# Every second expert's down projection as three single-pass products of high and low parts

## The chip, the core and the metric

The kernel runs on one NeuronCore of a Trainium2 chip. The metric is device time in microseconds from launch to end. TensorE (PE) multiplies, ScalarE (ACT) applies functions and copies, VectorE (DVE) and GpSimd (POOL) work elementwise, SyncE (SP) issues most of the transfers.

## What is computed

Eight sequences of 512 tokens with 128 features go through an attention layer and a mixture of experts, each followed by a residual sum and a layer norm:

```python
x = _layernorm(x + attention(x, w_qkv))            # 16 heads of 8
...
combine = ...                                      # top 8 of 16 experts, scaled, else 0
hg = jnp.einsum('bsd,eid->bsei', x, w_gate)
hu = jnp.einsum('bsd,eid->bsei', x, w_up)
h = jax.nn.silu(hg) * hu
ye = jnp.einsum('bsei,edi->bsed', h, w_down)
y = jnp.einsum('bsed,bse->bsd', ye, combine)
y = y + shared expert (gate, up, silu, down)
x = _layernorm(x + y)
```

All 16 experts are computed for every token and weighted with `combine`. All arithmetic is float32.

## The kernel before

There are two stages. The attention stage runs over the 8 batches and ends with the routing of the first batch; a barrier of all engines lies between the stages. The feed-forward stage (`feed_forward`) runs over 8 batches: `body` is written out for the first and the last, with a loop over the six between. Tiles have features or hidden units on the 128 partitions and the 512 tokens of a batch in the free dimension.

A batch has 18 steps (`STEPS`), 0 to 17. "Net" 0 is the shared expert, nets 1 to 16 are the experts. In step s:

- PE makes `gate` and `up` of net s (L1197), each as three matmuls of type fp32r, which PE takes in a single pass: low weights by high x, high weights by high x, high weights by low x. "High" is a value rounded to fp32r, "low" is the rest. Then it makes the down projection of net s - 4 (`LAG`, L1227), one float32 matmul into `ps_y`, which the trace shows as two records. The down projections of nets 14 to 16 come in steps 0 to 2 of the next batch.
- ACT turns `ps_gate` into `silu` (L1115).
- DVE multiplies it with `ps_up` (in PSUM) into `gated` (L1167).
- POOL multiplies `gated` with the routing weights into `hidden` (L1085); both inputs are in SBUF.

The other work of a batch is written between these by step number. DVE: moments of the next batch (step 0), its layer norm `x` (step 2, L305), the sum `y_sum` (step 6), routing in three parts (`select_experts`, steps 7, 9, 11), the layer norm `result` of the batch before (step 13, L305). POOL: `scale` (steps 1 and 7), a copy of x1 (step 3, L324). ACT: the copy of y (step 3), of x1T (step 5), `decay` (step 7, with two table loads), `combine_T` (step 14).

The end of a batch is a hand-over. After `up` of net 16, ACT rounds the transposed x1 of the next batch into `x1T_high` (L344, step 17); DVE then subtracts to get `x1T_low` (L349); PE meanwhile makes the down projections of nets 12 and 13, and then step 0 of the next batch, which is ordered so that four matmuls need only `x1T_high` and the fifth is the first to need `x1T_low`:

```python
if s == 0:
    pe.wait_ge(r.x1T_split, b + 1)
```

Each engine works through its own instructions in the order written, waiting on semaphores. The rings are `silu` and `gated` 3 deep, `hidden` 6 deep, `ps_gate` 2, `ps_up` 3.

Of the kernel before, what the change touches and what calls it, by code (L numbers as in the profile page):

```python
# [124 lines left out]
NETS = EXPERTS + 1  # L125
ROUTE_SCALE = 2.826
# [25 lines left out]
def build(nc, x, xT, w_qkv, w_nets, w_downs, gate_wT, expert_bias, out):  # L152
    q_rows = nc.dram_tensor("q_rows", [HEADS, ROWS, SEQ], F32).ap()
    k_rows = nc.dram_tensor("k_rows", [HEADS, ROWS, SEQ], F32).ap()
    shift_rows = nc.dram_tensor("shift_rows", [2, GROUP * TILES, P], F32).ap()
    combine_rows = nc.dram_tensor("combine_rows", [EXPERTS, SEQ], F32).ap()
    x_tiles = x.rearrange("b (t p) d -> p (b t) d", p=P)
    out_tiles = out.rearrange("b (t p) d -> p (b t) d", p=P)

    with ExitStack() as whole:  # L160
        def keep(name, shape, dt=F32):
            return whole.enter_context(nc.sbuf_tensor(name, shape, dt))


        stream = keep("stream", [P, BATCHES * TILES, HIDDEN])
        nets_high = keep("nets_high", [P, NETS, 2, P], F32R)
        nets_low = keep("nets_low", [P, NETS, 2, P], F32R)
        nets_down = keep("nets_down", [P, NETS, P])
        ident = keep("ident", [P, P])
        r = RouteState(nc, whole, combine_rows)  # L170
        c = ContextState(nc, whole)
        attention(nc, r, c, stream, nets_high, nets_low, nets_down, ident, x_tiles, xT, w_qkv,
                  w_nets, w_downs, gate_wT, expert_bias, q_rows, k_rows, shift_rows)
        feed_forward(nc, r, c, stream, nets_high, nets_low, nets_down, ident, out_tiles)


class RouteState:


    def __init__(self, nc, ctx, combine_rows):  # L180
# [36 lines left out]
        self.downs_loaded = sem("downs_loaded")  # L217
        self.moments_ready = [sem("moments_in"), sem("moments_out")]
# [216 lines left out]
def attention(nc, r, c, stream, nets_high, nets_low, nets_down, ident, x_tiles, xT, w_qkv,  # L435
              w_nets, w_downs, gate_wT, expert_bias, q_rows, k_rows, shift_rows):
    with ExitStack() as ctx:
# [167 lines left out]
        def _(pool):  # L605
# [39 lines left out]

            def body(b, first=False, last=False):
                for g in range(GROUPS):
# [15 lines left out]
                    if g == 3:  # L663
                        add_context(pool, c, stream, 2 * b, b, 0)
                    if first and g > 0:
                        split_net(g - 1)
                        load_net(g)
                    elif not first and not last and g in (1, 3):
                        split_net(2 * b + 1 + g // 2)
                        load_net(2 * b + 2 + g // 2)  # L670
                    elif last and g < 2:
                        split_net(NETS - 2 + g)
                        if g == 0:
                            load_net(NETS - 1)

# [318 lines left out]
def feed_forward(nc, r, c, stream, nets_high, nets_low, nets_down, ident, out_tiles):  # L994
# [6 lines left out]
    def before(s, ring):  # L1001
# [4 lines left out]
        return (0, n) if n >= 0 else (-1, n + STEPS)  # L1006

    with ExitStack() as ctx:  # L1008
# [14 lines left out]
        result = sb("result", [P, TILES, HIDDEN])  # L1023

# [10 lines left out]
        hidden_done = sem("hidden_done")  # L1035
        down_done = sem("down_done")
# [65 lines left out]
        def _(act):  # L1102
# [4 lines left out]

            def body(b, first=False, last=False):
                for s in range(STEPS):
# [6 lines left out]
                    if s == STEPS - 1 and not last:  # L1116
# [3 lines left out]
                        round_x1T(act, r)  # L1120

# [16 lines left out]
        def _(dve):  # L1138
# [13 lines left out]

            def gate_up(b, s, first):
# [15 lines left out]
            def body(b, first=False, last=False):  # L1169
                for s in range(STEPS):  # L1170
                    if s <= LAST:
                        gate_up(b, s, first)
                    if s == STEPS - 1 and not last:
                        split_x1T(dve, r, b + 1)
                    if s == LN_IN - 1 and not last:
# [20 lines left out]
        def _(pe):  # L1196
# [30 lines left out]
            def down(b, n, first):  # L1227
                if n == 0:
                    pe.wait_ge(gated_done, NETS * b + 1)
                    if not first:  # L1230
                        pe.wait_ge(y_copied, b)
                else:
# [29 lines left out]
            pe.wait_ge(r.downs_loaded, DMA)  # L1262
            turn_context(pe, c, ident, 2 * BATCHES - 1, 1, c.ps_turned)
# [39 lines left out]
```

## Time and profile before

| | |
|---|---|
| median of 3 runs | 723.49 us (723.25 to 724.71) |
| the profiled execution | 725.11 us, of which the span of its instructions is 723.4 us |
| granted TensorE clock, mean | 0.966 |
| busy in the span | PE 687.6, PE's weight loads 361.9, DVE 515.3, ACT 415.6, POOL 321.2 us |

Busy time is the union of an engine's instructions; the ends of matmuls are modelled. The chain that ended last is followed back from the last instruction, at each step to what released it; its pieces lie end to end, so their lengths are the time that each took on the path. A row of the timeline gives an instruction's start and its duration, waits inside the instruction included. The feed-forward stage begins at 393 us.

### The profile page before, as it was taken

The page shows a single profiled execution, that of the slowest core. Times are in us where ns is not written, and L with a number is a line of the kernel's source. Part 1 is how long each engine was busy: PE and PEld are TensorE (multiplying, and loading weights), DVE is VectorE, ACT ScalarE, POOL GpSimd, SP SyncE. Part 2 cuts the span into 40 slices and gives each one's busy share as a digit, 9 for nine tenths or more (in the row PEclk, how much of TensorE's full clock was granted, in tenths as well). Part 3 has the DMA queues.
Part 4 walks back from the last instruction along what each step waited for, and adds up shares of the span by engine and source line. Part 5 has one row for each costly group of instructions (what it writes and reads, how often), then busy time and mean ns, then how long its engine had stood idle before and what let it go on. Part 6 is the DMA issues. An engine that isn't in the chain of part 4 may idle for free. (4 is left out here: it accounts for less than half of the span.)

```text
span 723.4 us, 13286 instructions
## 1 busy us (share of the span) xinstructions
PE 687.6 (95%) x3494; PEld 361.9 (50%) x3494; DVE 515.3 (71%) x1085; ACT 415.6 (57%) x779; POOL 321.2 (44%) x371
## 2 busy tenths in 40 slices
PE   2899999999999999999997999999999999999995
PEld 1343333433434334343323767666676767676662
DVE  1889988999999999999953546557565655656343
ACT  2068877988879888787886424334343434334321
POOL 3033342423424252252230756665565646666563
PEclk8569999999999999999999999999999999999998
DMA  6832251422414233241105023050606032140600
GB/s 184 257 98 89 84 156 34 140 70 82 155 53 148 68 100 110 82 137 52 46 5 202 33 108 128 22 227 0 248 0 245 3 145 103 50 198 9 239 1 29
DMA packets 34279, 74.89 MB, mean 104 GB/s; under 512 B 4144, under 2 KB 13488, under 8 KB 30032
## 3 DMA queue, kind: packets, MB, share of 16 engines
q1 hardware_dynamic: 33440, 72.38, 29.1%
q0 software_dynamic: 816, 2.23, 1.1%
q8 instruction: 11, 0.18, 0.1%
q14 instruction: 12, 0.10, 0.0%
HBM read 58.61 MB, written 15.99 MB: 103 GB/s over the span
## 5 line engine op out<-in xcount | busy, mean ns | idle before, releaser
L743 ACT ACTIVATE probs<-ps_k 128x512 f32<-128x512 f32 x500 | 262.6, 605 | 51.7 <-PE ps_k L849 47.5
L786 DVE TENSOR_REDUCE maxima<-ps_bank 128x1 f32<-128x512 f32 x384 | 245.4, 682 | 27.5 <-PE ps_bank L842 22.4
L1085 POOL TENSOR_TENSOR hidden<-gated,weights 128x512 f32<-128x512 f32 x128 | 167.0, 1311 | 124.2 <-DVE gated L1167 108.4
L1115 ACT ACTIVATE silu<-ps_gate 128x512 f32<-128x512 f32 x136 | 81.3, 598 | 176.9 <-PE ps_gate L1209 176.6
L1167 DVE TENSOR_TENSOR gated<-silu,ps_up 128x512 f32<-128x512 f32 x128 | 87.0, 685 | 105.2 <-PE ps_up L1209 69.7
L842 PE MATMUL ps_bank<-k_aug,q_aug 32*128 32x512 f32 x384 | 147.9, 513 | 12.5 <-DMA q_aug<-q_rows 8.8
L849 PE MATMUL ps_k<-q_aug,k_aug 32*128 32x512 f32 x500 | 154.2, 489 | 4.0 <-ACT probs L743 2.2
L862 PE MATMUL ps_ctx<-probs,v_ones 128*32 128x512 f32 x1024 | 138.8, 614 | 0.9 <-ACT probs L743 0.9
L1234 PE MATMUL ps_y<-hidden,nets_down 128*128 128x512 f32 x272 | 137.1, 591 | 0.0
L849 PEld LDWEIGHTS ps_k<-q_aug,k_aug 32*128 32x128 f32 x500 | 64.0, 185 | 124.3 <-ACT probs L743 107.2
L1206 PE MATMUL ps_gate<-x1T_high,nets_low 128*128 128x512 f32 x136 | 96.5, 710 | 0.0
L618 POOL TENSOR_TENSOR shift<-shift_raw,ones 16x128 fp32r<-16x128 f32 x31 | 13.8, 445 | 180.5 <-ACT shift_raw L711 180.5
L786 DVE TENSOR_REDUCE maxima<-ps_turned 128x1 f32<-128x512 f32 x128 | 87.2, 681 | 3.5 <-PE ps_bank L842 1.9
L842 PEld LDWEIGHTS ps_bank<-k_aug,q_aug 32*128 32x128 f32 x384 | 61.0, 191 | 27.6 <-DVE maxima L786 14.8
L842 PE MATMUL ps_turned<-k_aug,q_aug 32*128 32x512 f32 x128 | 65.0, 508 | 1.3
L1234 PEld LDWEIGHTS ps_y<-hidden,nets_down 128*128 128x128 f32 x272 | 51.3, 189 | 15.6 <-issue 3.8
L1209 PE MATMUL ps_gate<-x1T_low,nets_high 128*128 128x512 f32 x136 | 53.6, 394 | 0.0
L1209 PE MATMUL ps_gate<-x1T_high,nets_high 128*128 128x512 f32 x136 | 53.6, 394 | 0.0
L1209 PE MATMUL ps_up<-x1T_low,nets_high 128*128 128x512 f32 x136 | 53.4, 393 | 0.0
L1206 PE MATMUL ps_up<-x1T_high,nets_low 128*128 128x512 f32 x136 | 53.2, 391 | 0.0
L1209 PE MATMUL ps_up<-x1T_high,nets_high 128*128 128x512 f32 x136 | 53.2, 391 | 0.0
L1209 PEld LDWEIGHTS ps_gate<-x1T_high,nets_high 128*128 128x128 f32 x136 | 25.8, 189 | 24.9 <-issue 24.5
(117 smaller groups left out, 648.9 us busy)
## 6 DMA issues: line engine op xcount, KB each, us to landing
weights<-combine_rows SPq DMA_DIRECT2D x32, 1024.0 KB, 7.5
k_aug<-k_rows SPq DMA_DIRECT2D x32, 256.0 KB, 2.7
q_aug<-q_rows SPq DMA_DIRECT2D x32, 256.0 KB, 2.9
q_rows<-qk_high SPq DMA_DIRECT2D x16, 256.0 KB, 2.9
k_rows<-qk_high SPq DMA_DIRECT2D x16, 256.0 KB, 3.6
net_raw<-w_nets POOLq DMA_DIRECT2D x17, 128.0 KB, 2.4
xT_sb<-xT SPq DMA_DIRECT2D x8, 256.0 KB, 2.9
q_rows<-qk_low SPq DMA_DIRECT2D x8, 256.0 KB, 3.1
```

The source lines that it names most:

```text
L618: pool.tensor_tensor(shift[:, 0, :], shift_raw[:], r.ones[0:GROUP * TILES, 0:P], ALU.mult).then_inc(shift_high, 1)
L743: act.activation(probs[:, t, h, :], score_slot(i, last)[:], ACT.Exp, scale=ATT_SCALE).then_inc(exp_done, 1)
L786: dve.tensor_reduce(maxima[:, parity, TILES * h + t:TILES * h + t + 1], bank("q", (i - UNIT * AHEAD) % SCORES)[:], AX_X, ALU.max).then_inc ...
L842: return pe.matmul(bank("q", (i - UNIT * AHEAD) % SCORES)[:], q_aug[rows, g, t * P:(t + 1) * P], k_aug[rows, g, :], start=True, stop=True) ...
L849: return pe.matmul(score_slot(i, last)[:], k_aug[rows, g, t * P:(t + 1) * P], q_aug[rows, g, :], start=True, stop=True).then_inc(scores_k, 1)
L862: last = pe.matmul(ps_ctx[32 * h:32 * (h + 1), :], v_ones[:, g, t, h, :], probs[:, t, h, :], start=opens, stop=closes)
L1085: pool.tensor_tensor(hidden[:, s % RING, :], gated[:, s % UP_RING, :], r.weights[:, e, :], ALU.mult).then_inc(hidden_done, 1)
L1115: act.activation(silu[:, s % UP_RING, :], ps_gate[s % 2][:], ACT.Silu).then_inc(silu_done, 1)
L1167: dve.tensor_tensor(dst, silu[:, s % UP_RING, :], ps_up[s % UP_RING][:], ALU.mult).then_inc(gated_done, 1)
L1206: pe.matmul(dst[:], nets_low[:, s, j, :], r.x1T_high[:], start=True, stop=False)
L1209: return pe.matmul(dst[:], nets_high[:, s, j, :], x[:], start=False, stop=stop)
L1234: pe.matmul(ps_y[:], nets_down[:, n, :], hidden[:, n % RING, :], start=n == 0, stop=n == LAST).then_inc(down_done, 1)
```

## The change

For the odd nets 1, 3, ..., 15 the down projection is made as `gate` and `up` are: three fp32r matmuls. That needs the weights and `hidden` of these nets in high and low parts.

```diff
+            def split_downs():
+                odd = nets_down[:, 1:, :].rearrange("p (j two) d -> p j two d", two=2)[:, :, 0, :]
+                ones = r.ones[:, 0:P].unsqueeze(1).to_broadcast([P, SPLITS, P])
+                pool.wait_ge(r.downs_loaded, DMA)
+                pool.tensor_tensor(downs_high[:], odd, ones, ALU.mult).then_inc(r.downs_high_made, 1)
+                pool.wait_ge(r.downs_high_made, 1)
+                pool.tensor_tensor(downs_low[:], odd, downs_high[:].bitcast(F32), ALU.subtract
+                                   ).then_inc(r.downs_split, 1)
...
+                    if last and g == 3:
+                        split_downs()
...
+    def splits(s):
+        n = s - 2
+        return n > 0 and n % 2 == 1
...
+            def round_hidden(b, n, first):
+                j = n // 2
+                act.wait_ge(hidden_done, EXPERTS * b + n)
...
+                act.copy(hidden_high[:, j % SPLIT_RING, :], hidden[:, n % RING, :]).then_inc(hidden_highs, 1)
...
                         round_x1T(act, r)
+                    if splits(s):
+                        round_hidden(b, s - 2, first)
...
+            def split_hidden(b, n):
+                j = n // 2
+                dve.wait_ge(hidden_highs, SPLITS * b + j + 1)
+                dve.tensor_tensor(hidden_low[:, j % SPLIT_RING, :], hidden[:, n % RING, :],
+                                  hidden_high[:, j % SPLIT_RING, :].bitcast(F32), ALU.subtract
+                                  ).then_inc(hidden_split, 1)
...
                         split_x1T(dve, r, b + 1)
+                    if splits(s):
+                        split_hidden(b, s - 2)
...
+                elif n % 2 == 1:
+                    j = n // 2
+                    high, low = hidden_high[:, j % SPLIT_RING, :], hidden_low[:, j % SPLIT_RING, :]
+                    pe.wait_ge(hidden_highs, SPLITS * b + j + 1)
+                    pe.matmul(ps_y[:], downs_low[:, j, :], high, start=False, stop=False)
+                    pe.matmul(ps_y[:], downs_high[:, j, :], high, start=False, stop=False)
+                    pe.wait_ge(hidden_split, SPLITS * b + j + 1)
+                    pe.matmul(ps_y[:], downs_high[:, j, :], low, start=False, stop=False).then_inc(down_done, 1)
+                    return
...
+            pe.wait_ge(r.downs_split, 1)
             turn_context(pe, c, ident, 2 * BATCHES - 1, 1, c.ps_turned)
```

`splits(s)` holds in the odd steps 3 to 17: ACT and DVE handle net s - 2 right behind their work on net s, two steps before PE's down projection of it. In step 17 ACT rounds `x1T_high` first and `hidden_high` of net 15 behind it.

PE, the first batch, step 5: the end of `up` of net 5, the down projection of net 1, the transposes of x1. Before:

```order
L1206 MATMUL ps_up<-x1T_high,nets_low 128x512
L1209 MATMUL ps_up<-x1T_high,nets_high 128x512
L1209 MATMUL ps_up<-x1T_low,nets_high 128x512
L1234 MATMUL ps_y<-hidden,nets_down 128x512
L331 MATMUL ps_route<-ident,x 128x128 x4
```

After:

```order
L1254 MATMUL ps_up<-x1T_high,nets_low 128x512
L1257 MATMUL ps_up<-x1T_high,nets_high 128x512
L1257 MATMUL ps_up<-x1T_low,nets_high 128x512
L1284 MATMUL ps_y<-hidden_high,downs_low 128x512
L1285 MATMUL ps_y<-hidden_high,downs_high 128x512
L1287 MATMUL ps_y<-hidden_low,downs_high 128x512
L338 MATMUL ps_route<-ident,x 128x128 x4
```

One float32 matmul has become three of fp32r, with the same neighbours.

DVE, the first batch, steps 11 to 17: the third part of the routing (`chosen` to `combine`), the `gated` of nets 12 to 16, and `x1T_low`. In the other batches `result` (4 instructions) stands behind `gated` of net 13 as well. Before:

```order
L393 TENSOR_TENSOR chosen<-struck,select 128x64
L395 TENSOR_TENSOR picked<-chosen,score 128x64
L397 TENSOR_REDUCE total<-picked 128x4
L399 RECIPROCAL inverse_total<-total 128x4
L401 SCALAR_TENSOR_TENSOR combine<-picked,inverse_total 128x64
L1167 TENSOR_TENSOR gated<-silu,ps_up 128x512 x5
L349 TENSOR_TENSOR x1T_low<-x1T,x1T_high 128x512
```

After, behind the subtraction of net 9:

```order
L400 TENSOR_TENSOR chosen<-struck,select 128x64
L402 TENSOR_TENSOR picked<-chosen,score 128x64
L404 TENSOR_REDUCE total<-picked 128x4
L406 RECIPROCAL inverse_total<-total 128x4
L408 SCALAR_TENSOR_TENSOR combine<-picked,inverse_total 128x64
L1213 TENSOR_TENSOR gated<-silu,ps_up 128x512 x2
L1195 TENSOR_TENSOR hidden_low<-hidden,hidden_high 128x512
L1213 TENSOR_TENSOR gated<-silu,ps_up 128x512 x2
L1195 TENSOR_TENSOR hidden_low<-hidden,hidden_high 128x512
L1213 TENSOR_TENSOR gated<-silu,ps_up 128x512
L356 TENSOR_TENSOR x1T_low<-x1T,x1T_high 128x512
```

Each subtraction (of nets 11 and 13 here) stands between `gated` of its step and the extra work of that step; the one of net 15 follows `x1T_low`.

## Rows read from the trace of the kernel before

**Rows 1.** The page: busy time; the granted PE clock in 40 slices.

```profile
PE 687.6 (95%) x3494; PEld 361.9 (50%) x3494; DVE 515.3 (71%) x1085; ACT 415.6 (57%) x779; POOL 321.2 (44%) x371
...
PEclk8569999999999999999999999999999999999998
```

**Rows 2.** The page: the chain that ended last, by engine.

```profile
PE 45%; DVE 0%; POOLq 0%; ACT 0%; issue 0%; DVEq 0%; POOL 0%
```

**Rows 3.** A stretch: its us, busy (x) of PE, PEld, DVE, ACT, POOL; clock.

```profile
440.00:720.00 280.00, 275.28 (x1053) 186.50 (x1052) 155.89 (x408) 99.07 (x158) 165.97 (x143) 1.00 0.25 97
```

**Rows 4.** The chain in order of time, 607 to 613 us: start, us, what.

```profile
610.68 0.86 PE ps_y L1234 x2
611.54 0.23 PE ps_gate L1206
611.78 0.47 PE ps_gate L1209 x2
...
612.94 0.86 PE ps_y L1234 x2
```

**Rows 5.** The chain, 590 to 634 us: two batch ends.

```profile
590.97 1.72 PE ps_y L1234 x4
...
602.18 0.86 PE ps_y L1234 x2
...
631.34 1.72 PE ps_y L1234 x4
```

**Rows 6.** Single lines: count, shortest, median and longest in ns.

```profile
L349 DVE TENSOR_TENSOR x1T_low<-x1T,x1T_high x8: 682/684/693, 377.6 to 672.5; 128x512 fp32r<-128x512 f32 x8
...
L344 ACT CAST x1T_high<-x1T x8: 610/618/618, 376.9 to 671.8; 128x512 fp32r<-128x512 f32 x8
...
L1085 POOL TENSOR_TENSOR hidden<-gated,weights x128: 1262/1290/1666, 398.4 to 711.2; 128x512 f32<-128x512 f32 x128
```

**Rows 7.** Timeline, 618 to 634 us: start, us, what.

```profile
620.47 0.22 DVE L393 TENSOR_TENSOR chosen<-struck,select 128x64 f32<-128x64 f32 x1
...
620.63 1.29 POOL L1085 TENSOR_TENSOR hidden<-gated,weights 128x512 f32<-128x512 f32 x1 [0.94 <-DVE gated L1167]
620.76 1.24 DVE L395 TENSOR_TENSOR picked<-chosen,score 128x64 f32<-128x64 f32 x1
...
622.89 0.69 DVE L1167 TENSOR_TENSOR gated<-silu,ps_up 128x512 f32<-128x512 f32 x1
...
624.96 2.09 DVE L305 TENSOR_SCALAR result<-y_sum,moments,scale 128x128 f32<-128x128 f32 x4
...
625.13 1.33 POOL L1085 TENSOR_TENSOR hidden<-gated,weights 128x512 f32<-128x512 f32 x1 [0.19 <-DVE gated L1167]
...
626.97 0.67 DVE L1167 TENSOR_TENSOR gated<-silu,ps_up 128x512 f32<-128x512 f32 x1
```

**Rows 8.** Timeline of VectorE, 626 to 640 us: the end of a batch.

```profile
631.54 0.69 DVE L1167 TENSOR_TENSOR gated<-silu,ps_up 128x512 f32<-128x512 f32 x1 [1.56 <-POOL hidden L1085]
632.14 0.68 DVE L349 TENSOR_TENSOR x1T_low<-x1T,x1T_high 128x512 fp32r<-128x512 f32 x1
```

**Rows 9.** Timeline of GpSimd, same stretch.

```profile
632.30 1.66 POOL L1085 TENSOR_TENSOR hidden<-gated,weights 128x512 f32<-128x512 f32 x1 [0.95 <-DVE gated L1167]
```

**Rows 10.** Timeline of ScalarE, 589 to 606 us: the copy of y.

```profile
600.64 0.58 ACT L1106 COPY yT<-ps_y 128x512 f32<-128x512 f32 x1
```

**Rows 11.** Timeline of VectorE and the chain at 403 us: the first batch.

```profile
402.95 1.87 DVE L1167 TENSOR_TENSOR gated<-silu,ps_up 128x512 f32<-128x512 f32 x3
...
403.00 0.86 PE ps_y L1234 x2
```

**Rows 12.** Timeline at 385 to 394 us, and the halving of a net.

```profile
385.25 0.72 POOL L278 TENSOR_TENSOR stream<-stream,context 128x256 f32<-128x256 f32 x1 [10.91 <-DVE context L267]
...
393.27 0.63 PE L253 MATMUL ps_turned<-ident,context_T 128*128 128x128 f32 x4 [1.11 <-PEq L437]
...
L641 POOL TENSOR_TENSOR nets_high<-net_raw,ones x17: 716/731/740, 58.5 to 362.2; 128x256 f32 x12, 128x256 fp32r<-128x256 f32 x5
```

More of the change, by code:

```diff
@@ L125 @@
 NETS = EXPERTS + 1
+SPLITS = EXPERTS // 2
+SPLIT_RING = 4
 ROUTE_SCALE = 2.826
@@ L168, in build @@
         nets_down = keep("nets_down", [P, NETS, P])
+        downs_high = keep("downs_high", [P, SPLITS, P], F32R)
+        downs_low = keep("downs_low", [P, SPLITS, P], F32R)
         ident = keep("ident", [P, P])
@@ L171, in build @@
         c = ContextState(nc, whole)
-        attention(nc, r, c, stream, nets_high, nets_low, nets_down, ident, x_tiles, xT, w_qkv,
+        attention(nc, r, c, stream, nets_high, nets_low, nets_down, downs_high, downs_low, ident, x_tiles, xT, w_qkv,
                   w_nets, w_downs, gate_wT, expert_bias, q_rows, k_rows, shift_rows)
-        feed_forward(nc, r, c, stream, nets_high, nets_low, nets_down, ident, out_tiles)
+        feed_forward(nc, r, c, stream, nets_high, nets_low, nets_down, downs_high, downs_low, ident, out_tiles)
 class RouteState:
@@ L217, in __init__ @@
         self.downs_loaded = sem("downs_loaded")
+        self.downs_high_made = sem("downs_high_made")
+        self.downs_split = sem("downs_split")
         self.moments_ready = [sem("moments_in"), sem("moments_out")]
@@ L432, in load_weights, with attention @@
                  ).then_inc(r.weights_loaded[i], DMA)
-def attention(nc, r, c, stream, nets_high, nets_low, nets_down, ident, x_tiles, xT, w_qkv,
+def attention(nc, r, c, stream, nets_high, nets_low, nets_down, downs_high, downs_low, ident, x_tiles, xT, w_qkv,
               w_nets, w_downs, gate_wT, expert_bias, q_rows, k_rows, shift_rows):
@@ L991, in _, with feed_forward @@
             weigh_values(UNITS - 1, GROUPS - 1, TILES - 1, None)
-def feed_forward(nc, r, c, stream, nets_high, nets_low, nets_down, ident, out_tiles):
+def feed_forward(nc, r, c, stream, nets_high, nets_low, nets_down, downs_high, downs_low, ident, out_tiles):
     STEPS = NETS + 1
@@ L1023, in feed_forward @@
         result = sb("result", [P, TILES, HIDDEN])
+        hidden_high = sb("hidden_high", [P, SPLIT_RING, SEQ], F32R)
+        hidden_low = sb("hidden_low", [P, SPLIT_RING, SEQ], F32R)
         ps_gate = [psum("ps_gate0", [P, SEQ]), psum("ps_gate1", [P, SEQ])]
@@ L1035, in feed_forward @@
         hidden_done = sem("hidden_done")
+        hidden_highs = sem("hidden_highs")
+        hidden_split = sem("hidden_split")
         down_done = sem("down_done")
@@ L1106, in copy_y @@
                 act.copy(yT[:], ps_y[:]).then_inc(y_copied, 1)
+            def round_hidden(b, n, first):
+                j = n // 2
+                act.wait_ge(hidden_done, EXPERTS * b + n)
+                if j >= SPLIT_RING:
+                    act.wait_ge(down_done, NETS * b + n - 2 * SPLIT_RING + 1)
+                elif not first:
+                    act.wait_ge(down_done, NETS * (b - 1) + n + 2 * (SPLITS - SPLIT_RING) + 1)
+                act.copy(hidden_high[:, j % SPLIT_RING, :], hidden[:, n % RING, :]).then_inc(hidden_highs, 1)
             def body(b, first=False, last=False):
```

## The prediction

> **What bounds the kernel now.** I read the page first: PE is busy 95% of the span, the other engines at most 71%, and its granted clock is at full speed in all slices of the second half [rows 1]. Busy alone proves nothing, since the ends of matmuls are modelled, so I went to the chain that ended last: PE holds it for 45% of the span, which is the whole feed-forward stage, and every other engine has 0% [rows 2]. By stretches, in the loop batches PE is busy 275.3 of 280 us at clock 1.00, DVE 155.9, ACT 99.1, POOL 166.0 [rows 3]. The chain in order of time shows a step without extras as PE work end to end: from one down projection to the next 612.94 - 610.68 = 2.26 us, of which the float32 product takes 0.86; the fp32r products behind it take 0.23 and, two together, 0.47 [rows 4]. A batch takes 631.34 - 590.97 = 40.37 us [rows 5]. So in this stage time taken from PE is time won, until another engine is late.
>
> **What the change removes and adds on PE.** 64 float32 down projections (8 nets, 8 batches) of 0.86 us become 64 times three fp32r products of the same shape as those of gate and up, 3 x 0.23 = 0.69 us [rows 4]. That is 0.17 a product, 1.36 a batch, 64 x 0.17 = 10.9 us. Both sides: if the three went at the rate of the slowest fp32r piece, 0.24, it would be 0.14 x 64 = 9.0 us; if the step's remainder, 2.26 - 0.86 = 1.40 for six, held a cost of 0.03 that comes only with the float32 neighbour, 0.20 x 64 = 12.8. I take 10.9, since the pieces are even. The two extra semaphore waits of each product cost nothing when satisfied: the first products of gate and up carry such waits too, and their pieces are 0.23 like the others.
>
> The Trainium skill (FP8 and Floating Point Precision, TensorE Precision Notes) says that true float32 takes four passes through the array. By that rule a pass here is 0.86 / 4 = 0.215 us, and three of these would save 13.8 us; the trace has fp32r products at 0.23, so I stay with the rows.
>
> **What it adds elsewhere.** *ACT*: 64 roundings of 0.62 us, as x1T_high [rows 6]. ACT is busy 99 of 280 us, and the rounding in step s waits for the hidden of net s - 2, which POOL normally finishes some 2 us before. Behind it are queued the copy of y (step 3), of x1T (step 5), decay (step 7) and the next silu. The tightest is the copy of y: it moves from 600.64 to about 601.0 and is done by 601.6, while PE's down projection of net 0, at 602.18 before, asks for it at 602.0 [rows 5, 10]. So zero. *DVE*: 64 subtractions of 0.68 us, as x1T_low [rows 6], 5.5 us on 22.5 a batch: it stays under the 39 us of a batch. *POOL*: the weights are halved once. 256 columns take 0.73 us [rows 12], 512 take 1.29 [rows 6], so 1024 about 1.29 + 2 x 0.56 = 2.4, twice that is 4.8 us. It starts when the sum at 385.25 ends, 385.97, and is done by 390.8; PE begins the new stage at 393.27 [rows 12]. Zero, with 2.5 us of cover; at twice the duration it would cost 2.4 us.
>
> **Where something can get late.** The subtraction reads two SBUF tensors, as POOL's multiply does, and these shut each other out. At 620.47 chosen, on 128x64, took 0.22 us; at 620.76 picked, of the same size, took 1.24, until POOL's hidden of 620.63 was over; at the end of a batch hidden took 1.66 instead of 1.29 beside x1T_low [rows 6 to 9]. The gated product has one input in PSUM and takes 0.67 to 0.69 throughout [rows 7, 8]. The Trainium skill (SBUF, State Buffer; SBUF: two separate sides) speaks of an exclusive lock that is held for the whole instruction, by a VectorE operation with two SBUF inputs or by a GpSimd one; the trace agrees, with the 1.24.
>
> *First batch.* Steps 0 to 3 have no down projections, so PE comes early to net 1: its product starts at 403.00 [rows 11], the third part at 403.46. On DVE gated of net 3 follows the layer norm of step 2 at 402.95 (three of them in 1.87, 0.62 apart), the subtraction of net 1 at 403.57, done at 404.25. With 0.07 for the signal (a gated to its hidden) PE stands until 404.3: **0.85 us lost, once**.
>
> *Ends of the batches 1 to 6*, the ones with routing, result and hand-over. Occupancy is about 0.62 for a gated or a subtraction, 1.25 for a POOL multiply. I assume that whoever waits gets the port when the holder is done: result at 624.96 let POOL in at 625.13 between its four parts [rows 7]. In the times of the trace at 618 to 632 us:
> - Step 11: PE is 5 x 0.17 = 0.85 ahead by the end of it, gated of net 11 starts at 619.2, and the subtraction of net 9 behind it is done by 620.7. That pushes the routing's last part behind POOL's multiply of net 11, 620.7 to 621.95. From there chosen and picked take 0.25 each and the rest the 0.89 that lay between the end of picked (622.0) and 622.89 [rows 7]: gated of net 12 comes at 623.35 instead of 622.89, and its hidden, 0.76 behind and 1.25 long, is done at 625.35.
> - Step 13: the subtraction of net 11 waits for that, ends 625.96; POOL takes net 13 until 627.2; only then result (0.8 for its rest); gated of net 14 at 628.0 instead of 626.97 [rows 7], its hidden 628.75 to 630.0.
> - Step 15: gated of net 15 at 628.6; the subtraction of net 13 waits until 630.0, done 630.65. PE asks for it at 632.20 + 0.46 - 7 x 0.17 = 631.47. In time.
> - Step 16, 17: gated of net 16 at 630.65 (PE's products are ready at 631.54 - 1.19 = 630.35 [rows 8]); POOL has net 15 from 630.65 to 631.9; x1T_low 631.9 to 632.58. PE asks for it after its two down projections and four products: 631.34 + 1.72 + 0.92 - 8 x 0.17 = 632.62 [rows 5]. Before, it had 1.16 us to spare (632.82 against 633.98); now none.
>
> So the stall is zero by the sum, but with no reserve. Each of a dozen handovers is good to some hundredths. I take 0.15 us in each of 6 batches, 0.9 us; the bounds are 0 and what the rivals give. The last batch has neither routing nor hand-over, and the tail behind PE's last product is unchanged.
>
> **Sum.** Against the profiled execution, 725.11 us (span 723.4 and 1.7 around it): 725.11 - 10.9 + 0.85 + 0.9 = 715.95, that is 9.15 less. It was 1.6 above the median of the runs; on the median, 723.49 - 9.15 = **714.3 us**.
>
> **Rivals.**
> 1. *The collisions cost a real stall at each hand-over*, 0.5 to 1.0 us in 6 batches, 3 to 6 us in place of 0.9. For it: no reserve, and one further collision (0.6 to 1.25 us) on the way from step 9 to 17 is enough. Against: once PE has lost 0.5 us, all that follows has 0.5 more. 716.4 to 719.4 us.
> 2. *POOL goes on with its next multiply while DVE waits* (two ready multiplies back to back keep the port). Then each subtraction of steps 9 to 15 lets two of them pass: net 9's ends at 623.1, routing gives gated of 12 and 13 by 625.8, multiplies 12 and 13 run until 627.8, the subtraction of net 11 until 628.4, result until 629.3, gated of 14 and 15 until 630.5, multiplies 14 and 15 until 632.55, the subtraction of net 13 until 633.2: 1.8 us after PE's 631.47, and x1T_low 0.2 more. 6 x 2.0 = 12.0 us: 723.49 - 10.9 + 0.85 + 12.0 = 725.4, **slower**. It decides from 1.7 us a batch ((10.9 - 0.85) / 6). Against: rows 7 show POOL let in between DVE's parts, which speaks for taking turns; no row shows DVE waiting with two multiplies ready.
> 3. *The three products take as long as the float32 one* (0.86): then 723.5 to 726, no gain. Against: the same form stands next to it at 0.23. For it only that ps_y takes all three accumulating, as ps_gate does.
> 4. *The step keeps only what the even rate gives*, 0.20 a product, and no stall: 723.49 - 12.8 + 0.85 = 711.5.
>
> **Chances.** Forecast with stalls under 0.4 us a batch (713.2 to 715.8): 0.50. Rival 1: 0.29. Rival 2: 0.06. Rival 3 or a partial form that ends within 0.2%: 0.05. Rival 4: 0.10. The range reaches from rival 4 past most of rival 1: 711.3 to 720.0. A measurement can tell about 0.2%, 1.4 us, from no change. Faster: 0.50 + 0.29 + 0.10 = 0.89; within: 0.05; slower: 0.06.
>
> **What the profile after would show.** In the chain, odd down projections as three pieces with 0.69 in sum, steps alternating 2.26 and 2.09, a loop batch of 39.0 to 39.2 us. One pause of about 0.85 us before the third product of net 1 in the first batch, put down to DVE. DVE subtractions at 0.68 where alone and up to 1.3 longer beside a multiply; hidden up to 0.6 longer. At each hand-over x1T_low ending within some tenths of PE's fifth product. A wait of PE on ACT, or a steady wait on hidden_low in the loop batches, would prove my schedule wrong; pieces of 0.29 would prove the product's price wrong.

## The result, and the profile after

| | before | changed | ratio (95% interval) |
|---|---|---|---|
| median of the runs made side by side, us | 724.1 (723.25 to 728.98) | 717.32 (716.75 to 719.25) | 0.9873 (0.9826 to 0.9919) |
| profiled execution, us (span) | 725.11 (723.4) | 717.01 (715.3) | |
| feed-forward stage, us | 723.4 - 393.27 = 330.1 | 715.3 - 394.38 = 320.9 | |
| loop batch, us | 40.37 | 39.07 | |

The changed kernel is 1.3% faster by the ratio; the two medians alone differ by 0.9%, and a second, longer series gave 1.05% (below). The forecast was 714.3 us, between 711.3 and 720.0. The stage is measured from its first transposes (the row of L253 in [rows 12], of L260 below) to the end of the span, the batch from one copy of y to the next.

The page after: busy time, the granted clock in 40 slices, and the chain by engine (answers to [rows 1, 2]).

```profile
PE 678.9 (95%) x3558; PEld 373.8 (52%) x3558; DVE 580.4 (81%) x1149; ACT 448.0 (63%) x843; POOL 348.0 (49%) x373
...
PEclk8569999999999999999999999999999999999998
...
PE 44%; DVE 1%; POOLq 0%; issue 0%; ACT 0%; DVEq 0%; POOL 0%
```

In a chain, "issue" is time in which the engine waited for nothing that the profile shows, and a q behind an engine's name stands for its sequencer. PE is still the chain, 8.7 us less busy, and DVE has 65 us more. The loop batches as one stretch (answers to [rows 3]; the stretch is 272 us, as the loop is shorter):

```profile
440.00:712.00 272.00, 267.16 (x1113) 197.30 (x1111) 214.15 (x465) 128.44 (x216) 185.85 (x143) 1.00 0.26 102
```

DVE went from 0.56 of the stretch to 0.79. That is much more than 64 subtractions of 0.68, as the single lines show (answers to [rows 6]; count, then shortest/median/longest in ns):

```profile
L1113 POOL TENSOR_TENSOR hidden<-gated,weights x128: 1267/1304/1752, 399.5 to 703.3; 128x512 f32<-128x512 f32 x128
```

```profile
L1195 DVE TENSOR_TENSOR hidden_low<-hidden,hidden_high x64: 677/1146/1779, 404.7 to 703.7; 128x512 fp32r<-128x512 f32 x64
```

The median subtraction takes 1.15 us, 0.68 alone. The rest is time beside POOL's multiply, which in turn takes 1.49 on average (1.31 before). The chain in order of time, in the batches of 600 to 630 us and where they meet (answers to [rows 4, 5]):

```profile
606.22 0.23 PE ps_y L1284
606.45 0.24 PE ps_y L1285
606.69 0.23 PE ps_y L1287
...
608.31 0.86 PE ps_y L1291 x2
```

```profile
627.38 0.23 PE ps_y L1287
627.61 0.23 PE ps_gate L1254
...
628.54 0.23 PE ps_gate L1257
```

An odd net's down projection is three pieces, 0.70 in sum, against 0.86 for the float32 one that is left. Between two batches no piece is longer than 0.23: PE does not wait. What comes ready for it there (timeline; answers to [rows 7 to 9]):

```profile
621.76 2.07 DVE L312 TENSOR_SCALAR result<-y_sum,moments,scale 128x128 f32<-128x128 f32 x4
...
624.50 4.68 POOL L1113 TENSOR_TENSOR hidden<-gated,weights 128x512 f32<-128x512 f32 x3 [1.53 <-DVE gated L1213]
624.95 1.40 DVE L1195 TENSOR_TENSOR hidden_low<-hidden,hidden_high 128x512 fp32r<-128x512 f32 x1
...
626.45 0.62 ACT L351 CAST x1T_high<-x1T 128x512 fp32r<-128x512 f32 x1 [0.44 <-DMA out<-result]
627.10 0.95 DVE L356 TENSOR_TENSOR x1T_low<-x1T,x1T_high 128x512 fp32r<-128x512 f32 x1 [0.15 <-ACT x1T_high L351]
```

Net 13's subtraction ends at 626.35, 1.03 ahead of PE's third product at 627.38. x1T_high ends at 627.07, 0.54 ahead of the product at 627.61, and x1T_low at 628.05, 0.49 ahead of PE's fifth at 628.54. x1T_high started only when the store of result had landed (the DMA in brackets). Three multiplies of POOL without a gap take 4.68, while DVE does its own subtractions in the same time: the two engines take turns. The first batch, a line of PE's timeline and the chain (answers to [rows 11]):

```profile
403.92 0.39 PE L1284 MATMUL ps_y<-hidden_high,downs_low 128*128 128x512 f32 x1
...
403.88 0.26 DVE x L312
404.14 0.59 DVE gated L1213
404.74 0.61 DVE hidden_low L1195
405.35 0.04 issue
405.39 0.50 PE ps_y L1287
```

Here is the pause of the forecast. PE's first product began at 403.92, so the third would have begun at about 404.38, two pieces of 0.23 later; it began at 405.39, 1.0 us late, and then took 0.50 in the chain, not 0.23. From the up projection ahead of it to the next gate PE loses 1.1 us in all (2.87 against 1.90 before, with 0.16 saved on the product). The expectations below have the pause as 1.05. Last, the halving of the weights ahead of the stage (answers to [rows 12]):

```profile
385.66 2.36 POOL L658 TENSOR_TENSOR downs_high<-nets_down,ones 128x1024 fp32r<-128x1024 f32 x1
...
388.10 2.36 POOL L660 TENSOR_TENSOR downs_low<-nets_down,downs_high 128x1024 fp32r<-128x1024 f32 x1
...
394.38 0.63 PE L260 MATMUL ps_turned<-ident,context_T 128*128 128x128 f32 x4 [1.11 <-PEq L444]
```

It ended at 390.46, 3.9 us ahead of the stage. Yet the stage began 1.1 us later than before. By stretches of 4 us the third number from the end, the granted clock, shows why:

```profile
384.00:388.00 4.00, 3.04 (x19) 0.93 (x23) 0.83 (x5) 1.34 (x4) 3.02 (x2) 0.74 0.04 8
388.00:392.00 4.00, 3.41 (x20) 0.53 (x12) 0.00 (x0) 3.30 (x7) 2.38 (x2) 0.83 0.84 324
```

A clock of 0.74 is a stretch spent in part at the lower level (1.2 GHz); a matmul on 32 rows at 386.98 took 0.79 us there, 0.50 otherwise. From the sum of the context on POOL at 384.98 to the start of the stage this execution takes 9.40 us; the kernel before takes 8.02, and so do six profiles below that have the halving in the same place and the clock at 1.00 there. Such episodes, some 3 us each, come in several places of attention and at the change of stage, and differ from execution to execution of one kernel. So whole times scatter by 3 us and more, and below I compare kernels by the length of the stage and the period of a batch, and give the whole time beside them. The period repeats to 0.1 us, and so does the stage where no such episode falls on its start; where one does, the table says so.

| run | nets in three passes | stage, us | loop batch, us | median, us | ratio to before (95%) |
|---|---|---|---|---|---|
| before | none | 330.1 | 40.37 | 724.1 | 1 |
| changed | 8 | 320.9 | 39.07 | 717.32 | 0.9873 (0.9826 to 0.9919) |
| changed, again | 8 | 320.8 | 39.07 | 718.25 | 0.9895 (0.9873 to 0.9917) |
| PE's part alone | 8 | 320.6, with 1.8 at the low clock | 38.95 | 712.77 | 0.9815 (0.9793 to 0.9838) |
| side work alone | none | 333.1, with 1.6 at the low clock | 40.36 | 727.73 | 1.0004 (0.9971 to 1.0038) |
| first order | 8 | 320.4 | 39.05 | 716.43 | 0.9873 (0.9842 to 0.9904) |
| subtraction on POOL | 8 | 340.1 | 41.33 | 736.59 | 1.0132 (1.0094 to 1.017) |
| net 15 first | 8 | 330.1 | 40.53 | 725.97 | 0.9996 (0.9961 to 1.0031) |
| two subtractions | 8 | 367.2, with 1.6 at the low clock | 44.5 to 47.1 | 765.15 | 1.0523 (1.0483 to 1.0562) |
| weights halved early | 8 | 320.9 | 39.07 | 715.87 | 0.9838 (0.9807 to 0.9869) |
| net 1 whole at first | 8 | 321.5, with 1.6 at the low clock | 39.07 | 721.41 | 0.9929 (0.99 to 0.9958) |
| ten nets | 10 | 320.3 | 39.16 | 721.63 | 0.9937 (0.991 to 0.9964) |
| twelve nets | 12 | 334.4 | 41.01 | 734.57 | 1.0109 (1.0064 to 1.0153) |
| fifteen nets | 15 | 354.8 | 44.37 | 754.72 | 1.0386 (1.0344 to 1.0427) |

Each ratio is to executions of the kernel before that were made beside that kernel's; from the third row on their median was 726.1 to 727.3 us, so a median of those rows is not to be set against 724.1. Ratios leave out executions in a slow state of the chip, some per cent longer at a lower clock; the profiled one of PE's part alone, 723.44 us, was such.

### The profile page after: what moved, and what is told of

Same layout as the page of the kernel before. It is cut to its first block and busy times, and to the rows that moved or that the text cites. A ratio compares the mean times of both kernels' runs of the same rounds, so it can differ in the third digit from the quotient of the medians.

```text
span 715.3 us, 13700 instructions
## 1 busy us (share of the span) xinstructions
PE 678.9 (95%) x3558; PEld 373.8 (52%) x3558; DVE 580.4 (81%) x1149; ACT 448.0 (63%) x843; POOL 348.0 (49%) x373
## 5 line engine op out<-in xcount | busy, mean ns | idle before, releaser
L1113 POOL TENSOR_TENSOR hidden<-gated,weights 128x512 f32<-128x512 f32 x128 | 189.1, 1493 | 93.1 <-DVE gated L1213 79.5
L861 PE MATMUL ps_bank<-k_aug,q_aug 32*128 32x512 f32 x384 | 147.6, 510 | 11.9 <-DMA q_aug<-q_rows 8.3
L1254 PE MATMUL ps_gate<-x1T_high,nets_low 128*128 128x512 f32 x136 | 74.7, 550 | 0.0
L1195 DVE TENSOR_TENSOR hidden_low<-hidden,hidden_high 128x512 fp32r<-128x512 f32 x64 | 71.5, 1117 | 2.8 <-ACT hidden_high L1143 1.3
L1291 PE MATMUL ps_y<-hidden,nets_down 128*128 128x512 f32 x144 | 73.4, 591 | 0.0
L1143 ACT CAST hidden_high<-hidden 128x512 fp32r<-128x512 f32 x64 | 39.4, 616 | 8.7 <-POOL hidden L1113 8.7
```

Source lines behind the costliest of these rows:

```text
L861: return pe.matmul(bank("q", (i - UNIT * AHEAD) % SCORES)[:], q_aug[rows, g, t * P:(t + 1) * P], k_aug[rows, g, :], start=True, stop=True) ...
L1113: pool.tensor_tensor(hidden[:, s % RING, :], gated[:, s % UP_RING, :], r.weights[:, e, :], ALU.mult).then_inc(hidden_done, 1)
L1195: dve.tensor_tensor(hidden_low[:, j % SPLIT_RING, :], hidden[:, n % RING, :], hidden_high[:, j % SPLIT_RING, :].bitcast(F32), ALU.subtract ...
L1254: pe.matmul(dst[:], nets_low[:, s, j, :], r.x1T_high[:], start=True, stop=False)
L1291: pe.matmul(ps_y[:], nets_down[:, n, :], hidden[:, n % RING, :], start=n == 0, stop=n == LAST).then_inc(down_done, 1)
```

## The experiments

**The changed kernel again**, unedited.

> The changed kernel once more, for a tighter ratio. Theory A (all of the gain is PE's: 64 products shorter by 0.16 us, less about 1.0 us lost once in the first batch): 715.5 to 717.5 us, a loop batch of 39.1 us. Theory B (the gain is partly the draw of that one execution): 719 us or more.

713.61 to 719.49 us in six runs; stage and batch as in the first profile. The profiled execution was the one of 713.61, with the stage begun at 391.06, against 394.38: 3.3 of the 3.4 us of difference to the first profile lie ahead of the stage. Of these, 1.8 had come about by the first sum of the context of the second batch, at 112.25 against 114.06, and 1.4 lie in the episode at the end; what the first part comes from was not followed.

**PE's part alone.** The three products take constants as operands; there is no rounding, no subtraction and no halving, so the down projections of odd nets are left out of the result.

```diff
-                    pe.wait_ge(hidden_highs, SPLITS * b + j + 1)
-                    pe.matmul(ps_y[:], downs_low[:, j, :], high, start=False, stop=False)
+                    pe.wait_ge(hidden_done, EXPERTS * b + n)
+                    pe.matmul(ps_y[:], nets_low[:, n, 0, :], stand_in, start=False, stop=False)
...
-                        round_hidden(b, s - 2, first)
...
-                        split_hidden(b, s - 2)
...
-                        split_downs()
```

> PE's part alone: odd down projections are three fp32r products on constant operands (the weights and x of gate and up in place of the down weights and hidden), each behind hidden alone; no rounding, no subtraction, the down weights are not halved. Theory A: 10.3 us off the kernel before (64 x 0.16), 1.0 less than the changed kernel, batch 39.08 as there, no pause in the first batch. Theory B (rounding and subtraction also cost PE in the loop batches): a loop batch under 38.9 us and over 2 us less than the changed kernel. The start of the stage, 1.1 us later in the changed kernel's profile, is back at 393.3 if halving the weights was its cause.

The batch is 38.95 us, 1.42 below before: 0.178 a product. The changed kernel saves 1.30, 0.163 a product. In its profile the stage began at 401.14, at a clock of 0.50: from the first transposes to the first down projection 9.1 us, where other kernels take 7.3. Without these 1.8 the stage is 318.8 us, 2.1 less than in the changed kernel, of which 0.7 is in the loop and the rest at the two ends. The whole time is 5.5 us less than that of the changed kernel in the same series, where I had put 1.0 less. The other 3.4 us would lie in the attention stage, where this kernel differs only by the halving that it leaves out. Whether they come from that is open; the run with the weights halved early bears on it. In the loop PE is busy without any gap:

```profile
440.00:704.00 264.00, 264.00 (x1107) 196.76 (x1106) 154.58 (x403) 99.62 (x160) 164.38 (x142) 1.00 0.29 115
```

**The side work alone.** Rounding, subtraction, halving and their waits stay; the product is the float32 one.

```diff
                     pe.wait_ge(hidden_highs, SPLITS * b + j + 1)
-                    pe.matmul(ps_y[:], downs_low[:, j, :], high, start=False, stop=False)
-                    pe.matmul(ps_y[:], downs_high[:, j, :], high, start=False, stop=False)
                     pe.wait_ge(hidden_split, SPLITS * b + j + 1)
-                    pe.matmul(ps_y[:], downs_high[:, j, :], low, start=False, stop=False).then_inc(down_done, 1)
-                    return
```

> Everything but the three products: rounding, subtraction, halved weights and the two waits are there, PE makes its one float32 product behind both waits. Theory A (the side work is hidden): kernel before plus 1.2 to 1.6 us, all of it the pause at net 1 in the first batch, which now falls before the whole product; loop batches 40.37. Theory B (the side work costs by itself): loop batches over 40.5 us, 2 us or more in all.

A loop batch is 40.36 us, before 40.37: in the loop the side work is free. The stage is 3.0 us longer, but 1.6 of that is not the edit's: it began at a low clock (granted 0.68 in 392 to 396 us), and from the first transposes to the first down projection takes 8.9 us where the kernel before takes 7.3. The pause at net 1 is 1.1 us: from that projection to the transposes of x1 4.2 against 3.1. About 0.5 comes at the very end, from the down projection of net 12 to the copy of y (5.0 against 4.5). There the chain has this, where the whole product waits for a subtraction that the three-part one needs only for its third piece:

```profile
711.27 1.70 POOL hidden L1113
...
712.99 0.63 ACT hidden_high L1143
...
713.65 1.68 DVE hidden_low L1195
...
715.46 1.97 PE ps_y L1286 x4
```

Without the low clock the stage is 1.4 us longer, in the 1.2 to 1.6 that I had expected, though I had put all of it at net 1. In the changed kernel the last third product loses only 0.15, so the order of the three products, low weights and high weights first and the late operand last, is worth some 0.3 us there. As 0.12 us a batch separates the changed kernel from PE's part alone, and the side work costs nothing beside a float32 product, this 0.12 comes with the products' own operands and waits; that is inferred, no run parts the two.

**The first order.** In the first batch the layer norm of x is put behind the gated of step 3 and its subtraction.

```diff
-                    if s == LN_IN + 1 and not last:
+                    if s == (LN_IN + 2 if first else LN_IN + 1) and not last:
```

> In the first batch alone the layer norm of x moves from step 2 to step 3 on DVE, behind gated of net 3 and the subtraction of net 1. Theory A (PE's pause at net 1 is the layer norm, 1.97 us, standing ahead of the subtraction): the pause of 1.05 us before the third product of net 1 goes, the kernel is 1.0 us faster than the changed one, loop batches stay at 39.1. Theory B (the pause comes from the port or from ACT's rounding): the pause stays, no change.

The pause before the third product is gone, but the stage gained only 0.4 to 0.5 us where I had expected 1.0. The chain shows what came in its place: the layer norm, now beside two multiplies of POOL, takes 2.97 us, not 1.97, and is late for the transposes of x1.

```profile
402.46 0.60 DVE x L312 x2
...
403.19 0.63 PE ps_route L338 x4
```

**The weights halved early**, in the second group of the last attention units, not in the fourth.

```diff
-                    if last and g == 3:
+                    if last and g == 1:
                         split_downs()
```

> The down weights are halved two units earlier in the last attention batch (about 360 us instead of 385.7). Theory A (the halving is hidden where it stands, and the differences of the stage's start, 391.1 to 394.4 us, come from episodes of lower clock): same times as the changed kernel, lowest run 713 to 714, median 716 to 719. Theory B (at 385.7 it slows the end of the attention stage or triggers an episode): median 3 to 5 us less, 712 to 714, like the kernel without halving.

The stage is unchanged, 320.95 us, as the halving was hidden before. Its median is lower than that of both series of the changed kernel (715.87 against 717.32 and 718.25), and the interval of its ratio overlaps that of the first and ends just under that of the second (0.9869 against 0.9873). My Theory B had 712 to 714 us, Theory A 716 to 719; the median lies between them, so whether the early place helps is open.

**The subtraction on POOL.**

```diff
+            def split_hidden(b, n):
+                j = n // 2
+                pool.wait_ge(hidden_highs, SPLITS * b + j + 1)
+                pool.tensor_tensor(hidden_low[:, j % SPLIT_RING, :], hidden[:, n % RING, :],
+                                   hidden_high[:, j % SPLIT_RING, :].bitcast(F32), ALU.subtract
+                                   ).then_inc(hidden_split, 1)
```

> The subtraction of odd nets is made by POOL, behind its multiply of the same step, instead of by DVE. POOL and DVE then collide no more often than before the change. Theory A (in the loop batches collisions fall on slack and cost PE nothing): loop batch 39.08 us as in the changed kernel; the pause in the first batch grows from 1.05 to about 3 us, since there POOL's multiply of net 3 comes first; stage 2 us longer than the changed kernel's 320.9. Theory B (collisions cost): loop batches shorter than 39.0.

The expectation missed for the loop. A batch takes 41.33 us: POOL leads the chain, and PE waits for it in the loop. (The pause in the first batch came as expected: the transposes of x1 begin 2.9 us later than in the kernel before, counted from the start of the stage.)

```profile
POOL 17%; PE 16%; issue 10%; ACT 1%; DVE 1%; POOLq 1%; DVEq 0%; ACTq 0%
```

```profile
440.00:720.00 280.00, 270.86 (x1114) 196.96 (x1112) 171.10 (x401) 127.91 (x215) 232.25 (x197) 1.00 0.26 103
```

POOL is busy 232 of 280 us, 0.83, and still decides: behind its subtraction stand the multiply of the next net and the chain gated, hidden, rounding, subtraction. VectorE was the right engine.

**Net 15 first.** ScalarE rounds hidden of net 15 ahead of x1T, not behind it.

```diff
+                    if s == STEPS - 1:
+                        round_hidden(b, s - 2, first)
                     if s == STEPS - 1 and not last:
                         act.wait_ge(up_ready, NETS * (b + 1))
```

> In step 17 ACT rounds hidden of net 15 first and x1T behind it. Theory A (the order matters, since ACT waits there for POOL's multiply of net 15): x1T_high ends 0.5 us after the rounding of net 15, PE waits about 1.0 us for it at the start of each of 7 batches, loop batch 40.1 us, stage 328 us. Theory B (PE's own work covers either order): loop batch 39.1, stage 321.

Seven waits of PE, one at each hand-over, and the chain of one:

```profile
PE ps_gate L1256 <- ACT x1T_high L351: 7.4, 7, 1.2
```

```profile
547.30 1.75 POOL hidden L1113
...
549.59 0.62 ACT x1T_high L351
...
550.35 0.49 PE ps_gate L1256
```

A batch takes 40.53 us, 1.46 more than in the changed kernel (expected about 1.0 more), and the stage 330.1: **the whole gain is gone**. ScalarE, busy for under half of the loop, stood at the rounding of net 15 until POOL's multiply was done, and x1T_high, ready to go, stood behind it.

**Two subtractions** for each, the first into a spare tile.

```diff
                 dve.wait_ge(hidden_highs, SPLITS * b + j + 1)
+                dve.tensor_tensor(spare[:, j % SPLIT_RING, :], hidden[:, n % RING, :],
+                                  hidden_high[:, j % SPLIT_RING, :].bitcast(F32), ALU.subtract)
```

> DVE makes each subtraction twice, the first into a spare tile. Theory A (DVE's work at the end of a batch has a reserve of 0.5 us for x1T_low and 1.0 for hidden_low of net 13, and no more): loop batches 40.0 to 41.5 us, the wait of PE is for x1T_low or hidden_low at the hand-over, and 0.6 more in the first batch; stage 328 to 337 us. Theory B (DVE has room, 214 of 272 us busy): loop batches stay at 39.1, stage 321.5.

```profile
PE ps_y L1290 <- DVE hidden_low L1198: 28.8, 26, 2.0
```

```profile
440.00:720.00 280.00, 253.19 (x1015) 179.38 (x1014) 249.08 (x479) 119.67 (x198) 175.95 (x129) 0.99 0.26 100
```

44.5 to 47.1 us a batch, where I expected 40.0 to 41.5. DVE is busy 0.89 of the stretch. Each subtraction more takes 1.4 to 1.8 us here, not 0.68: the cost of an operation that shares the port is that of its neighbour too.

**Net 1 whole at first.** Net 1 of the first batch keeps the float32 product. This kernel and the three that follow all do so; they take their nets from a list, halve all fifteen down weights, and halve them early.

```diff
-                    if splits(s):
+                    if splits(s) and not (first and s == 3):
...
-                elif n % 2 == 1:
+                elif n in SPLIT and not (whole and n == 1):
```

> The changed kernel, but the first batch's product for net 1 is one float32 product again (without the rounding on ScalarE and the subtraction on VectorE for that net in that batch); all fifteen down weights are halved, one group of token weights earlier. My theory: the 1.05 us that TensorE stands at net 1's third piece in the first batch goes, and the product costs 0.86 - 0.69 = 0.17 us more, so the feed-forward stage is about 0.9 us shorter than the 320.9 us of the changed kernel, 320.0 us, with the loop's batches still at 39.07 us. The rival: the layer norm of x1 is what the first batch really waits for, as in the run with the first order, and TensorE then stands at the transposes of x1; the stage stays at 320.4 to 320.9 us.

The stage is 721.8 - 400.29 = 321.5 us, but its first 4 us ran at a clock of 0.57, where seven matmuls took 0.43 instead of 0.23 and the transposes 0.81 instead of 0.63: 1.6 us, without which it is 319.9, as expected (320.0). From the second net's first up product to the router's gate, the stretch of the chain that holds the edit, it takes 415.14 - 404.57 = 10.57 us, and 407.76 - 396.26 = 11.50 in the kernel with the weights halved early: 0.93 less, expected 1.05 - 0.17 = 0.88. The whole time is worse all the same: 5.5 us above that of the kernel with the weights halved early. Two waits in 364 to 384 us, the stage before, tell where:

```profile
DVE x L313 <- POOL scale L306: 6.0, 1, 6.0
...
PE ps_bank L339 <- DVE context L275: 5.2, 1, 5.2
```

```profile
363.09 4.56 POOL L659 TENSOR_TENSOR downs_high<-nets_down,ones 128x2048 fp32r<-128x2048 f32 x1
367.73 4.56 POOL L661 TENSOR_TENSOR downs_low<-nets_down,downs_high 128x2048 fp32r<-128x2048 f32 x1
```

```profile
376.00:380.00 4.00, 1.87 (x8) 0.92 (x12) 1.88 (x8) 0.59 (x1) 2.03 (x3) 0.59 0.02 4
380.00:384.00 4.00, 4.00 (x22) 0.68 (x14) 0.69 (x1) 2.09 (x4) 0.00 (x0) 0.56 0.00 0
```

Twice the weights take POOL twice the time, 9.1 us. The layer norm's scale behind them comes late, and PE stands 5.2 us where it stood 1.2 with eight nets halved. All four kernels that halve fifteen nets have this wait of 5.2. Then the clock is at its lower level for the next matmuls, and the next stretch of attention, from one sum of the context on POOL to the next, takes 11.9 to 12.5 us in these four, against 10.5 at full clock. That the idle time brings this is not shown: most of the kernels that halve eight nets or none, and stood 1.2 us there, fall to the lower level in that place too and take 11.7 to 12.0; three (subtraction on POOL, net 15 first, weights halved early) do not. With eight nets halved there, this kernel would have a stage 0.9 us shorter than the changed one and nothing lost ahead of it; that version was not run.

**Ten, twelve, fifteen nets.** Against the kernel with net 1 whole the list of nets alone differs.

```diff
-SPLIT = [1, 3, 5, 7, 9, 11, 13, 15]
+SPLIT = [1, 2, 3, 5, 6, 7, 9, 11, 13, 15]
```

> As the run before in this job, with ten nets in three passes (the odd ones, 2 and 6). My theory: each net more saves TensorE 0.163 us and asks VectorE for one more subtraction of 0.68 to 1.4 us and ScalarE for one more rounding; x1T_low had 0.49 us to spare, so a batch is 39.07 - 0.33 = 38.75 us and the stage 320.0 - 8 x 0.163 = 318.7 us. The rival: VectorE has nothing left, as when its subtractions were doubled, and TensorE stands where a net follows a net in three passes: a batch of 39.1 us or more.

39.16 us a batch and a stage of 320.3, 0.4 longer than with eight nets in this form (319.9 without the low clock); 38.75 was expected, and the rival's side came true, though not by its wait. The chain, and the timelines of VectorE and ScalarE, at a hand-over:

```profile
513.33 0.12 issue
513.45 0.49 PE ps_gate L1260
```

```profile
507.99 2.08 DVE L313 TENSOR_SCALAR result<-y_sum,moments,scale 128x128 f32<-128x128 f32 x4
```

```profile
512.68 0.62 ACT L352 CAST x1T_high<-x1T 128x512 fp32r<-128x512 f32 x1 [0.96 <-DMA out<-result]
```

PE's first product of the new batch takes 0.12 + 0.49 instead of 0.23, so 0.38 is lost, and 39.16 - 0.38 = 38.78. DVE finishes result at 507.99 + 2.08 = 510.07, 3.26 ahead of PE's need at 513.33; with eight nets it was 621.76 + 2.07 = 623.83, 3.78 ahead of 627.61. By this half a us the store lands later, ScalarE rounds x1T later by as much, and the 0.54 us to spare is used up. A late VectorE shows here as a DMA and then as ScalarE. The wait for the store guards the buffer of result; whether the rounding could stand ahead of it, and ten nets then gain, was not run.

> Twelve nets in three passes (the odd ones, 2, 6, 10 and 14). If TensorE alone decided, a batch would take 39.07 - 4 x 0.163 = 38.42 us. VectorE's part: two subtractions a net in the run with doubled subtractions (eight more a batch) made a batch 5.4 to 7.6 us longer; four more should make it about 1 us longer than 38.42, 39.4 us, and the stage 322 to 324 us, which is slower than the eight nets of the changed kernel. The rival: ten and twelve nets are both hidden, 38.4 us.

41.01 us a batch (the first of the loop 42.6), 1.6 above the 39.4 expected: my price per subtraction was again too low. PE waits 1.4 us a batch for x1T_low, and 0.3 to 0.4 for x1T_high:

```profile
PE ps_gate L1263 <- DVE x1T_low L357: 8.2, 6, 1.4
PE ps_gate L1260 <- ACT x1T_high L352: 1.9, 6, 0.4
```

> All fifteen nets in three passes. TensorE alone: 39.07 - 7 x 0.163 = 37.93 us a batch. VectorE has seven subtractions more, nearly as many as the doubled ones, so it should be the bound: 42 to 45 us a batch, the stage 345 to 365 us, slower than the kernel before. The rival, in which VectorE keeps up: 38 us a batch and a stage of 312 us.

44.37 us a batch and a stage of 354.8, both as expected. PE now also waits in the middle of a batch:

```profile
PE ps_y L1293 <- DVE hidden_low L1201: 11.1, 12, 1.3
PE ps_gate L1263 <- DVE x1T_low L357: 10.3, 7, 1.5
```

Eight nets, every second one, is the best of the four numbers that were run; ten in this order give nothing more, and from twelve on PE waits for VectorE.

## Why the prediction was right

- **PE bounds, and its time is won.** Right. PE's part alone saves 1.42 a batch, and the side work alone leaves a loop batch at 40.36 against 40.37.
- **0.17 a product, 10.9 us.** Measured 0.163, 10.4 us, inside the bounds of 0.14 and 0.20; the pieces are 0.23 and 0.24. The Trainium skill (FP8 and Floating Point Precision, TensorE Precision Notes) gives four passes for float32; by that a pass is 0.86 / 4 = 0.215 us, an estimate, and three would cost 0.65; the rows have 0.70.
- **The first batch, 0.85 once.** It stood where I put it, and VectorE came as I put it: the subtraction ended at 404.66 + 0.68 = 405.34, and the stage had begun 1.1 later, so 404.25 had been right. But PE lost 1.1 us; the term was 0.25 too small. What it lacked is that the product behind the wait takes 0.50 in the chain and not 0.23. Net 1 left whole gave 1.1 - 0.17 = 0.93 back; moving the layer norm gave only 0.4, since PE needs that too.
- **Hand-overs, 0.15 in each of 6.** Too high: no wait in any. I had x1T_low end with nothing to spare at PE's fifth product, and it had 0.49; net 13's subtraction had 1.03, where I had 0.82. Ten nets, with 0.38 lost a batch, show how near it was.
- **Roundings on ScalarE cost nothing.** Right, and only because x1T is rounded ahead of net 15. I named the copy of y as the tightest, and it is: done at 596.84 + 0.59 = 597.43, it is 0.45 ahead of PE, where I had 0.4. Next comes x1T_high, 0.54 ahead of PE and behind a store of result that I had not followed; it is the one that gave way with ten nets.

```profile
596.84 0.59 ACT L1134 COPY yT<-ps_y 128x512 f32<-128x512 f32 x1
...
597.88 0.86 PE ps_y L1291 x2
```

- **Halving, 4.8 us, hidden.** Right in its duration, 4.80, and nothing waits for it. Twice the duration, at another place, cost 5 us of the whole time; at the old place I had put 2.4, by its own terms 385.97 + 9.6 - 393.27 = 2.3. That PE's part alone, without the halving, is 3.4 us shorter ahead of the stage stays open.
- **Sum.** In the profiled executions the stage is 9.2 us shorter, forecast 9.15. By terms: 10.4 won, 1.1 lost in the first batch and about 0.15 at the last third product, 9.15. That the two sums agree so closely is luck: 0.5 too much won and 0.25 too little lost in the first batch are made up by 0.9 set down for hand-overs that cost nothing, against the 0.15. The lower end that I gave for no stall, 713.2, should have been 714.3 - 0.9 = 713.4. The median came out at 717.32, 3 us above the forecast. The profiled execution is 1.1 us above the sum, and that is the later start of its stage, by the low clock ahead of it. My sum took the place where the stage begins as given, and held no term for its scatter from execution to execution.
- **Rival 1**, collisions of 3 to 6 us: the whole time lies in its interval, and yet it did not happen, as no hand-over has a stall. A number alone would have confirmed the wrong story.
- **Rival 2**, POOL keeps the port: fell. Two ready multiplies took 2.98 us in the changed kernel, where two alone take 2.5, with a subtraction of DVE let in between. Its mechanism, DVE too late for PE, is what twelve nets bring.
- **Rival 3**, no cheaper: fell with the pieces of 0.23. **Rival 4**, 0.20: PE's part alone came to 0.178.

## What to carry to other kernels

Where one engine is the chain and the others stand at 60%, work can be moved off it until the first of them has no time left at the one point where both meet; find that point in the timeline (here the hand-over and the copy of y, 0.5 us to spare), not in the busy shares. Count an operation that shares a port at its time beside the neighbour, 1.15 and not 0.68, and price the neighbour's delay too. And look at the order on the idle engine: a rounding put ahead of another on ScalarE, busy under half of the loop, was worth the whole 9 us.

## What the runs showed of the hardware

- VectorE and GpSimd take turns at operations with two SBUF inputs. Two ready multiplies of 128x512 take 2.98 us with a subtraction of VectorE between their starts, 2.49 for two without; a subtraction that meets one takes 1.4 to 1.78, alone 0.68. The layer norm, which reads one tensor in SBUF and its mean and scale, is held up too: a part of 128x128 takes 0.34 us, one beside a multiply 1.19 to 1.34.
- A product of 512 columns behind a wait takes 0.49 to 0.50 us of the chain, one behind another product 0.23 (the first batch, net 15 first, ten nets).
- An idle stretch of TensorE of 5.2 us was followed by matmuls at the lower clock for several us (0.59 and 0.56 granted in the two stretches of 4 us). The same place of attention shows the lower clock behind a wait of 1.2 us in some profiles and not in others.
- Six executions of the changed kernel lay between 713.61 and 719.49 us; the profiled one of them and that of the first series differ by 3.3 us ahead of the feed-forward stage and by 0.1 in it.
- Three fp32r products of 128x512 take 0.70 us, a float32 one, which the chain counts as two pieces, 0.86.
